# A last projection put into other PSUM banks, and a bias folded into the rows it is added to

## The reference

```python
def reference(x, ...):
    h = tok(x)                                   # linear attention with a token gate, PReLU
    h = h + attn(layernorm(h))                   # attention over the batch axis, gated, Wo, bo
    h = h + ffn(layernorm(h))                    # mixture of depths
    return h

def ffn(x, wr, br, w1, b1, w2, b2):              # x: (batches, 4096, 256)
    weights = x @ wr + br                        # one score per token
    k = 2048
    _, idx = top_k(weights, k)
    sel = idx[:, :k - 1]                         # the best 2047 tokens of each batch
    y = gelu(x[sel] @ w1 + b1) @ w2 + b2
    y = y * weights[sel]
    return scatter(zeros, sel, y) + x            # with the residual: h + x + y*weight
```

## Time and profile before

| | us |
|---|---|
| median of 3 runs | 2031.94 (2031.43 to 2033.35) |
| the profiled execution's own time | 2031.88 |
| its span in the profile | 2030.2 |
| PE busy | 1968.6 (97%) |
| DVE busy | 1221.4 (60%) |
| ACT busy | 691.1 (34%) |
| POOL busy | 455.6 (22%) |
| mean granted clock of TensorE | 0.987 |

### The profile page before, as it was taken

One profiled execution on the slowest core, in us unless ns is written; L12 is line 12 of the kernel. 1 busy time (PEld: TensorE's weight loads), 2 busy tenths in 40 slices (PEclk: granted clock), 3 DMA queues, 4 the chain that ended last, 5 costly groups with the idle time before them and its releaser, 6 DMA issues.

```text
span 2030.2 us, 27454 instructions
## 1 busy us (share of the span) xinstructions
PE 1968.6 (97%) x9494; PEld 1629.8 (80%) x9494; DVE 1221.4 (60%) x2229; ACT 691.1 (34%) x1119; POOL 455.6 (22%) x582
## 2 busy tenths in 40 slices
PE   8999999999999999999999999999999999939998
PEld 7788888888888888888888888888887888828897
DVE  5646565665656566766565656565565548867553
ACT  5422222222222225522222222222223537625554
POOL 4202020202102022420120202021120347623442
PEclk9999999999999999999999999999999999959999
DMA  4232433333242433233424333333424659721110
GB/s 156 85 108 83 152 113 125 115 124 126 91 166 96 143 113 127 83 104 125 155 72 160 123 116 113 124 107 122 145 84 155 213 183 313 271 67 57 43 43 32
DMA packets 87843, 250.14 MB, mean 123 GB/s; under 512 B 11697, under 2 KB 32177, under 8 KB 87729
## 3 DMA queue, kind: packets, MB, share of 16 engines
q1 hardware_dynamic: 83296, 240.26, 35.1%
q0 software_dynamic: 3072, 8.44, 1.3%
q10 hardware_dynamic: 1360, 0.01, 0.0%
HBM read 194.05 MB, written 54.62 MB: 122 GB/s over the span
## 4 chain that ended last, share of the span: by engine, by line
PE 91%; DVE 3%; issue 2%; ACT 2%; DMA 1%; POOL 0%; SPq 0%; DVEq 0%; ACTq 0%; POOLq 0%
PE bank L676 35%; PE bank L691 35%; PE bank L1637 5%; PE bank L834 4%; PE bank L1658 4%; PE bank L1206 2%; PE bank L646 1%; PE bank L722 1%; PE bank L620 1%; PE bank L630 1%; PE bank L723 1%; DVE kt L490 1%; PE bank L661 1%; PE bank L860 1%; DVE vf L501 0%
## 5 line engine op out<-in xcount | busy, mean ns | idle before, releaser
L691 PE MATMUL bank<-x_hi,kt 128*128 128x512 f32 x2048 | 723.9, 395 | 1.5 <-DVE work L528 1.4
L528 DVE SCALAR_TENSOR_TENSOR work<-bank,d_col,gate 128x512 f32<-128x512 f32 x512 | 383.9, 750 | 553.4 <-PE bank L691 544.3
L405 ACT ACTIVATE p_hi<-work 128x512 fp32r<-128x512 f32 x512 | 324.0, 633 | 1065.4 <-PE bank L676 1020.5
L691 PEld LDWEIGHTS bank<-x_hi,kt 128*128 128x128 f32 x2048 | 384.4, 188 | 90.4 <-DVE work L528 2.5
L676 PE MATMUL bank<-p_hi,v_hi 128*128 128x512 f32 x1024 | 407.0, 397 | 0.3 <-ACT yT L367 0.2
L676 PE MATMUL bank<-p_hi,v_lo 128*128 128x512 f32 x1024 | 404.1, 395 | 0.0
L676 PE MATMUL bank<-p_lo,v_hi 128*128 128x512 f32 x1024 | 403.4, 394 | 0.0
L691 PE MATMUL bank<-x_lo,kt 128*128 128x512 f32 x1024 | 400.9, 391 | 0.0
L516 DVE TENSOR_TENSOR p_lo<-work,p_hi 128x512 fp32r<-128x512 f32 x512 | 367.6, 718 | 29.3 <-ACT p_hi L405 29.2
L579 POOL TENSOR_SCALAR spread<-mv 128x4 f32<-128x4 f32 x16 | 3.9, 243 | 1124.5 <-DVE mv L459 1124.5
L676 PEld LDWEIGHTS bank<-p_hi,v_hi 128*128 128x128 f32 x1024 | 192.2, 188 | 50.6 <-DVE p_lo L516 5.3
(11 more groups left out here) (235 smaller groups left out, 2325.0 us busy)
## 6 DMA issues: line engine op xcount, KB each, us to landing
gate<-in_gateT SPq DMA_DIRECT2D x256, 512.0 KB, 3.6
work<-in_xT SPq DMA_DIRECT2D x32, 512.0 KB, 5.1
scratch_rows<-rows SPq DMA_DIRECT2D x16, 518.0 KB, 3.8
scratch_h<-work SPq DMA_DIRECT2D x16, 512.0 KB, 3.0
scratch_mn<-mn_sb SPq DMA_DIRECT2D x16, 512.0 KB, 6.7
scratch_mT_hi<-mT_hi SPq DMA_DIRECT2D x16, 512.0 KB, 2.7
scratch_mT_lo<-mT_lo SPq DMA_DIRECT2D x16, 512.0 KB, 4.0
gate<-scratch_mn SPq DMA_DIRECT2D x16, 512.0 KB, 4.3
```

The lines of the kernel that those rows point to most:

```text
L405: nc.scalar.activation(p_hi[:, i % 2, :], p32[:, i % RP, :], ACT.Copy).then_inc(hi_done, 1)
L528: nc.vector.scalar_tensor_tensor(p32[:, i % RP, :], S[i % 2][:, :], d_col[:, i:i + 1], gate[:, g % RG, j, :], ALU.add, ALU.mult).then_inc( ...
L691: mm = pe.matmul(S[i % 2][:, :], w, x, start=n == 1, stop=n == 3 * KD)
```

## The change

1. PE's projection of n = 14 goes into banks 4 to 7 (`last_products`), those of the values and gates of the last chunk. It waits until these are read (`o_ok`, `g_ok`) in place of the moments of n = 13. The projection of n = 15 stays in banks 0 to 3, and waits for the moments of n = 13, which were the last to read them, in place of those of n = 14.
2. On DVE, at the step c = 8, `route` of n = 13 stands behind `moments` of n = 14, no longer ahead of them.
3. In the last unit b2 is no longer added to the product. Four new instructions, one behind each of the `act_lo` of the steps j = 4 to 7, add `b2 * w_br` to the rows of `taken`; after the last matmuls one instruction for each tile forms `product * w_br + taken` straight out of PSUM. The first two of them wait for tiles 0 and 1 (`y_last` at 1), the others for tiles 2 and 3 (`y_last` at 2). `keep_y` and `give` of the last unit go.

```diff
+def pr_banks_from(pr, i):
+    return pr.psum[:, i * CH:(i + TPC) * CH].rearrange("p (j n) -> p j n", j=TPC)
 def mix(pr, W2, M, products, room, scratch, router, mlp_raw, W3, L):
...
         last = {}
+        last_products = pr_banks_from(pr, 4)
+        def products_at(c, s):
+            return last_products if (c, s) == (NC - 1, 0) else products
...
                 past(dve, st_x[s][h], c // 2 * 32)
+                products = products_at(c, s)
...
                 if within(c):
                     mixed(c, 0)
-                if within(c, 2) and c - 2 < NC - 1:
+                if within(c, 2) and c < NC:
                     route(c - 2, h, 1)
                 if within(c, 1):
                     moments(c - 1, 1 - h, 0)
+                if c == NC:
+                    route(c - 2, h, 1)
...
             def project(c, h, s):
                 n = c * 2 + s
                 pe.wait_ge(ogl_ok, c * 4 + 3 + s)
-                past(pe, h2_ok, n * 2)
-                past(pe, raw_ok, n)
+                products = products_at(c, s)
+                if (c, s) == (NC - 1, 0):
+                    pe.wait_ge(o_ok, NC * 4)
+                    pe.wait_ge(g_ok, NC * 4)
+                else:
+                    of = n - 1 if c == NC - 1 else n
+                    past(pe, h2_ok, of * 2)
+                    past(pe, raw_ok, of)
...
+            def weigh_b2(j):
+                dve.wait_ge(base_ok, U)
+                dve.wait_ge(wb_ok, U + 2)
+                row = taken[:, (U - 1) % HELD, j, 0:D]
+                nc.vector.scalar_tensor_tensor(row, b2[:, 0, :], w_br[:, (U - 1) % 2, j:j + 1], row,
+                                               ALU.mult, ALU.add).then_inc(b2_ok, 1)
...
                     if j == 3:
                         weigh(u)
+                    if u == U - 1 and 4 <= j:
+                        weigh_b2(j - 4)
...
-            keep_y(U - 1)
-            give(U - 1)
+            dve.wait_ge(st_out[(U - 1) % 2], (U - 1) // 2 * TPC * 16)
+            for i in range(TPC):
+                if i % 2 == 0:
+                    dve.wait_ge(y_last, i // 2 + 1)
+                j, h = i, (U - 1) % 2
+                dve.wait_ge(b2_ok, i + 1)
+                nc.vector.scalar_tensor_tensor(out_sb[:, h, j, :], YB[j // 2][:, (j % 2) * D:(j % 2 + 1) * D],
+                                               w_br[:, h, j:j + 1], taken[:, (U - 1) % HELD, j, 0:D],
+                                               ALU.mult, ALU.add).then_inc(out_ok, 1)
...
+                    if (u, j) == (U - 1, FT - 1) and t % 2 == 1:
+                        mm.then_inc(y_last, 1)
+                if (u, j) == (U - 1, FT - 1):
+                    return
                 mm.then_inc(y_done, 1)
```

More of the change, by code:

```diff
@@ L1444, in mlp @@
         x_ld = [[pr.sem(f"ff_x_ld{h}{j}") for j in range(TPC)] for h in range(HELD)]
+        y_last, b2_ok = pr.sem("ff_y_last"), pr.sem("ff_b2_ok")
         st_out = [pr.sem(f"ff_st_out{h}") for h in range(2)]
@@ L1700, in build @@
         psum = ps(nc, ctx, "bank", (P, 8 * CH))
+        pr.psum = psum
         banks = pr.banks = [psum[:, i * CH:(i + 1) * CH] for i in range(8)]
```

## The result

The changed kernel took 2028.47 us (median of 17 runs, 2026.55 to 2030.17), the kernel before 2031.78 beside it (17 runs, 2030.98 to 2034.74): a ratio of 0.9981, 95% interval 0.9974 to 0.9987. The forecast was 2028.0 in a range of 2026.8 to 2029.8. The medians differ by 3.3 us (0.16%), and the ratio lies 0.19% under 1, just short of the 0.2% that the prediction took as the least to be told from no change; its interval, 0.13 to 0.26%, doesn't include 1.

The account below looks back on a forecast made before the run. Bound by PE, busy 97% of the span, with a slack-free DVE and PE chain from the search's start to the gather. Gains 2.0 + 1.9 = 3.9 us off 2031.88 gave 2027.98, forecast 2028.0, range 2026.8 to 2029.8.

Parts of the forecast that it names:

- the idle gap of 1.1 us: PE in front of the projection of n = 14: idle 1.1 us in place of 3.09.
- 1.65 and 0.41: Before the search: 1.65 us from the end of n = 14's moments to line 1086, 0.41 more to the memset.
- a head of 1784.15 - 1774.87 = 9.28 us: From DVE's last og_lo (1774.87) to the search's memset, predicted at 1784.15 in place of 1786.35, a gain of 2.20 us.
- The middle value: Start of the search: gain taken as 2.0 us, between 1.75 (DVE held by POOL's power) and 2.20 (not held).
- the rival: The held route: DVE's route instructions wait for POOL's power, so 3.65 us gained, 2028.3; chance 0.28.
- the row of line 1087: DVE product of 4 columns, 0.156 us at best, 1.26 in the median beside POOL's 128x512 products; basis for the hold.
- fell to 0.51 from 1779 to 1782: PE's granted clock in the old product of n = 14, which took 4.30 us; 3.10 expected at full clock.
- could exceed 2.20 only if POOL's 1.65 shrank: Upper limit on the search-start gain: above 2.20 us only if POOL's stretch before the search got shorter.
- 1.20 and 0.71: Last unit, parts of the 1.91 us gain: 1.20 for the two instructions of y, 0.71 for half the last matmuls.
- the bound of 0.75 from line 528: First out_sb out of PSUM: 0.750 us for 512 columns bounds it from above, cutting the tail gain to 1.65.
- the slower rival: Last unit: four new instructions take 3.32 us each, overrun their gaps, cost 4.7 us of PE, 2032.7; chance 0.02.
- the predicted 3.9: Total gain in us: 2.0 at the start of the search plus 1.9 in the last unit.

Follow-up runs that it names:

- held: Six more VectorE 128x4 multiplications, both inputs in SBUF, behind the route of n=13, against the changed kernel; og_lo to memset 9.32 us (9.20), time 2027.06 us.
- after_fill: Eight idle matmuls in TensorE's gram-stage wait, against the changed kernel; mean 2028.32 us, 6 runs at 2027.05 to 2027.78, 4 at 2029.00 to 2030.36.

## Why the prediction was right, and where it was off

**PE.** Its start 0.73 us after the start of og_lo (measured 0.74), the idle gap of 1.1 us (1.13) and the full clock came as said; 48 matmuls followed without a gap.

**DVE.** The moments took 2.95 and 2.92 us, not 3.02. The rest, 1.65 and 0.41, was right to 0.1. The full working gave a head of 1784.15 - 1774.87 = 9.28 us; measured 9.21.

**The middle value.** What was off is the step "I take the middle, 2.0". It paid 0.2 for a hold that does not happen. w_mid of n = 14 took 0.22 us at 1784.46, and the power began 0.16 later; so the changed kernel's profile alone says little on the rival. The run named held does: even beside the power nothing of VectorE is held, only the power is stretched, by 0.12. The prediction carried the row of line 1087 over from a GpSimd product of 128x512 to one of 128x4. The Trainium skill (SBUF — State Buffer, Who interferes with whom) says that one of the two is blocked for the whole instruction; the runs agree for the wide products (1.26 us for the product of line 1099 that is otherwise 0.16) and not for the power (six products in 0.57 us beside it). It is the power that gives way, and not only in held. Over the kernel before:

```profile
L1165 POOL TENSOR_TENSOR rows<-spread,power x16: 1041/1267/1275, 1667.9 to 1819.9; 128x4 f32<-128x4 f32 x16
```

Thirteen of the sixteen run beside an og_lo of 128x512, which has both inputs in SBUF, and take 1.26 to 1.28 us; the other three take 1.04 to 1.05.

**One draw of the old head.** The larger miss is in what the gain was taken from. The prediction read "fell to 0.51 from 1779 to 1782" in one execution and took the 11.48 us for the kernel's. Three profiles of that head have 11.48, 11.82 and 12.69, mean 12.00, since the place of the fall varies; the new head has 9.20 to 9.21 in five. The gain is 2.3 to 3.5 us, 2.79 by the means, and a part of it (0.4 to 1.6, the step to 11.06) is the clock that no longer falls there. The bound "could exceed 2.20 only if POOL's 1.65 shrank" was wrong for this reason; the 1.65 itself stayed (1784.04 to 1785.69).

**The tail.** 1.9 predicted, 1.86 measured, and its two parts, 1.20 and 0.71, were 1.16 and 0.70. An out_sb straight out of the banks takes 0.476 us in the mean, and the same operation out of SBUF took 0.478 in the kernel before, so the source cost nothing, as chosen; the bound of 0.75 from line 528 did not come near. The four new instructions took 0.48 each, and the waits of the act_lo behind them, 1.73 to 1.75, still end with ScalarE. Nothing of the slower rival is seen.

**The sum.** By the traces 2.79 + 1.86 = 4.65 us in the mean. All runs together: 2032.72 before (mean of 70, three sessions) and 2028.27 after (mean of 28, two sessions), a difference of 4.45 +- 0.57 (95%). In the two sessions that have both kernels it is 3.9 +- 0.4 and 5.0 +- 0.4 (standard errors). So the predicted 3.9 was some 0.6 short, at the edge of that interval, and the 3.3 us of the medians shows less than was gained. The forecast of 2028.0 for a median that came out at 2028.47, and 2027.83 the second time, was right with a sum that was too small against a start that was, by mean, 0.8 higher than the 2031.94 it stood on: the mechanism held, but that the number fits so well is in part luck, two misses that cancel.

**What stays open.** Why TensorE's clock falls or not after the same gap of 1.99 us, what decides when it rises at the program's start and where it falls behind the gram stage, and what the upper level of after_fill is.

## What to carry to other kernels

When a stall of TensorE is taken from one profile, look whether its clock falls behind it: the gap of 3.09 us here cost 0.4 to 1.6 us more by the clock, depending on the execution, so take the price from several profiles and fill or shorten the gap. Two edits that look separate can need each other: here the order alone gained nothing in its one profile, in which the clock fell, the banks alone 0.4 to 1.6 us, both 2.3 to 3.5. Where the times of a kernel lie in groups, compare stretches of the traces and means over many runs, not medians of a few.

## What the runs showed that I had not expected

TensorE's clock after its 3.09 us in front of the old product fell in four of four profiles, after 1.13 us in none of nine; after the 1.99 us in the gram stage in eight of eleven, and in none of three with the gap filled. At the program's start eight matmuls of 128x256 took 3.76 us or 1.97 us, while the granted clock of the stretch reads 1.00 in both: the trace has no record there before its first, of full clock at 15.7 or 9.8 us, and the durations, not the column, show the pace. Behind the gram stage the clock fell at matmuls of two columns although TensorE ran them without a gap. And GpSimd's power of 128x4 does not hold VectorE's products with both inputs in SBUF, but six of them lengthened it by 0.12 us, and it is 0.22 to 0.23 us longer wherever it starts beside a VectorE operation of 128x512 with both inputs in SBUF.
